# K's chunks with the first fold block and seven variance tiles between them, the constant row's steps beside M's blocks, and another order of the loop's prologue

## The reference

```python
# layer 0
c   = einsum('bct,bcd->bdt', x, W[cond])                 # a 64x64 matrix picked per batch
q   = c @ Wq.T;  router: top 8 of 256 keys, softmax      # aux_out = probs @ aux_values @ Wvd.T @ Wvu.T
u   = clip(0.5 * log1p(var(c)) / mean(log1p(var(c))) + 2.5 * sigmoid(gelu(c @ Wu1.T + bu1) @ Wu2.T), 0, 5)
x1  = x + c + gate(u) * aux_out
# layer 1
r   = x1 @ base_weight.T + base_bias + (x1 @ A[id].T) @ B[id].T
out = x1 + r @ W_base.T + b_base + 0.5 * fourier(sum over 3 experts of masked coefs @ enc @ r)
```

## Time and profile before

| | |
|---|---|
| median of 3 runs | 1653.04 us (1652.23 to 1653.7) |
| the profiled execution's own time | 1652.13 us |
| its span | 1650.3 us |
| PE busy | 1596.8 us, 97% |
| DVE, ACT, POOL busy | 726.9, 587.6, 402.9 us |
| granted PE clock, mean | 0.985 of full speed |

### The profile page before, as it was taken

The page is one execution under the profiler, slowest core; times in us unless marked ns, Lnnn a source line. Parts: engine busy times, 40 slices in busy tenths (PEclk is TensorE's granted clock), DMA queues, the critical chain, the costliest instruction groups (busy, mean ns, idle before and its releaser), DMA issues.

```text
span 1650.3 us, 26441 instructions
## 1 busy us (share of the span) xinstructions
PE 1596.8 (97%) x7690; PEld 1324.9 (80%) x7690; DVE 726.9 (44%) x2497; ACT 587.6 (36%) x1269; POOL 402.9 (24%) x219
## 2 busy tenths in 40 slices
PE   5898999889999999999999999999999999999998
PEld 2676888668888888888888888888888888888886
DVE  3887555544433333333344433333443333433333
ACT  2333343333333333333333333333333333333332
POOL 2787777211111111111111111111111111111110
PEclk9799999999999999999999999999999999999999
DMA  9466655522222322223222222222222222222221
GB/s 338 141 212 215 184 184 167 176 62 86 86 86 89 90 86 84 85 87 91 88 86 84 84 84 84 84 84 84 84 84 84 84 84 84 84 85 85 86 69 49
DMA packets 160287, 176.46 MB, mean 107 GB/s; under 512 B 104654, under 2 KB 123041, under 8 KB 160138
## 3 DMA queue, kind: packets, MB, share of 16 engines
q1 hardware_dynamic: 158498, 170.98, 34.2%
q10 hardware_dynamic: 1768, 5.24, 0.9%
HBM read 136.69 MB, written 39.32 MB: 107 GB/s over the span
## 4 chain that ended last, share of the span: by engine, by line
PE 90%; POOL 3%; issue 3%; DVE 2%; DMA 1%; ACT 1%; SPq 0%; POOLq 0%; DVEq 0%; ACTq 0%
PE pair L1173 43%; PE pair L74 10%; PE pair L75 9%; PE pair L76 9%; PE pair L1142 6%; PE pair L1150 5%; POOL v_lo L220 3%; PE pair L1116 1%; PE pair L1191 1%; PE pair L1190 1%; PE pair L1198 1%; DMA w_kinds<-w_kinds_sb 1%; PE pair L1131 1%; POOL blk_lo L582 1%; PE pair L1121 0%
## 5 line engine op out<-in xcount | busy, mean ns | idle before, releaser
L1173 PE MATMUL pair<-m_hi,t_xt_hi 128*128 128x512 f32 x1024 | 332.4, 406 | 0.0
L1173 PE MATMUL pair<-m_lo,t_xt_hi 128*128 128x512 f32 x1024 | 322.6, 396 | 0.0
L1173 PE MATMUL pair<-m_hi,t_xt_lo 128*128 128x512 f32 x1024 | 321.9, 395 | 0.0
L1018 POOL TENSOR_TENSOR t_narrow<-t_a_raw,t_narrow 128x256 fp32r<-128x256 f32 x64 | 46.8, 731 | 1109.4 <-ACT t_xt_hi L926 1109.4
L1173 PEld LDWEIGHTS pair<-m_hi,t_xt_lo 128*128 128x128 f32 x1024 | 192.6, 188 | 47.0
L1173 PEld LDWEIGHTS pair<-m_lo,t_xt_hi 128*128 128x128 f32 x1024 | 192.5, 188 | 45.9
L1173 PEld LDWEIGHTS pair<-m_hi,t_xt_hi 128*128 128x128 f32 x1024 | 180.5, 189 | 34.3
L220 POOL TENSOR_TENSOR v_lo<-v_x,v_hi 128x1024 fp32r<-128x1024 f32 x64 | 159.6, 2504 | 74.9 <-ACT v_hi L214 74.8
L74 PE MATMUL pair<-t_narrow,t_xt_hi 128*128 128x352 f32 x512 | 177.8, 347 | 0.0
L75 PE MATMUL pair<-t_narrow,t_xt_hi 128*128 128x352 f32 x512 | 169.5, 331 | 0.0
L76 PE MATMUL pair<-t_narrow,t_xt_lo 128*128 128x352 f32 x512 | 168.5, 329 | 0.0
(11 more groups left out here) (218 smaller groups left out, 2650.3 us busy)
## 6 DMA issues: line engine op xcount, KB each, us to landing
v_x<-in_x SPq DMA_DIRECT2D x64, 512.0 KB, 3.5
t_xt<-in_x_t SPq DMA_DIRECT2D x64, 512.0 KB, 3.3
out<-t_out_sb SPq DMA_DIRECT2D x64, 512.0 KB, 2.7
t_rhs_b<-bk_hi SPq DMA_DIRECT2D x256, 64.0 KB, 2.3
t_a_raw<-in_lora_a SPq DMA_DIRECT2D x128, 64.0 KB, 2.9
t_bd<-w_kinds SPq DMA_DIRECT2D x128, 64.0 KB, 2.3
t_rhs_c<-bk_lo SPq DMA_DIRECT2D x128, 64.0 KB, 2.2
blk_raw<-in_left_blocks SPq DMA_DIRECT2D x12, 512.0 KB, 4.0
```

What stands on the lines that cost most here:

```text
L1018: pool.tensor_tensor(lora_groups(p, 1), b["a_raw"][:, p], f(lora_groups(p, 0)), ALU.subtract)
L1173: last = pe.matmul(pm_ps[:, c], lhs, m[:, k, c], start=a, stop=z)
```

## The change

1. **Setup.** `k_chunk` uses a single PSUM pair; its two halves and the two halves of `k_sum` signal separately. Between K's chunks PE now does the products of the first fold block (`first_block(k)`, with its result in the other pair) and variance tiles 2 to 8. `cs_hi` stands on ACT ahead of `v_hi` of tile 2. SP's loads are reordered: x of tiles 2, 3 and 4 and the first two left blocks are loaded here. Tile 9's split and block 0's evacuation are at the end of the lists of setup.
2. **Fold.** Blocks 1 to 11 remain, with tile numbers as before. The constant row's steps are beside M's blocks, two in each, after the second and the fourth tile; blocks 1 to 3 have none.
3. **Prologue.** PE forms the constant row after two of the eight `v_chunks`; ACT places it before the splits of Wu1 and Wq; DVE does `a_low(0)` and `a_low(1)` first, the constant row's low part before the router operands, and `wa_split` last. A memset of `rhs_c` moves from DVE to POOL.

```diff
@@ setup, SP
+        load_picked_w(0)
+        load_picked_w(1)
         load_two(kf, "w_base_t", 0, wbase_in)
+        load_rows(2)
+        sp.dma_start(f_["blk_raw"][:], left_block(t, 0)).then_inc(f_["raw_loaded"], 16)
+        load_picked_w(2)
+        load_two(kf, "w_base_t", 1, wbase_in)
         sp.wait_ge(s["w_kinds_ready"], 2)
         sp.dma_start(t["w_kinds"].rearrange("n c k d -> c n k d"), f(w_kinds[:])
                      ).then_inc(g["w_stored"], 16)
+        load_rows(3)
...
+        sp.wait_ge(f_["blo_ready"], 1)
+        sp.dma_start(f_["blk_raw"][:], left_block(t, P * HID)).then_inc(f_["raw_loaded"], 16)
         sp.wait_ge(g["w_stored"], 16)
...
@@ setup, ACT
-        var_hi(act, v, 2, 3, 0, 1)
         act.wait_ge(s["cs_mm_done"], 1)
         act.mul(cs_hi[:], cs_ps[0:RENC, :], 0.5).then_inc(s["cs_hi_ready"], 1)
-        for k in range(KC):
+        rows_high(2)
+        k_high(0)
+        block_high(0)
+        rows_high(3)
+        for k in range(1, KC):
             k_high(k)
...
+            if k >= 3:
+                rows_high(k + 1)
@@ setup, POOL
+        k_low(0)
+        rows_low(3)
+        for k in range(1, KC):
             k_low(k)
...
+            if k >= 3:
+                rows_low(k + 1)
...
@@ setup, PE
         def k_chunk(k):
+            e = slice(k * P, (k + 1) * P)
+            for h, c in enumerate((LEFT, RIGHT)):
+                if k == 0:
+                    pe.wait_ge(s["enc_cs_split"], 2)
+                else:
+                    pe.wait_ge(f_["k_sum_ready"], 2 * k - 1 + h)
+                product3(pe, k_ps[:, c], enc_hi[:, e], enc_lo[:, e], cs_hi[:, c], cs_lo[:, c], True, True
+                         ).then_inc(f_["k_mm_done"], 1)
+
+        def first_block(k):
...
+            for c in (LEFT, RIGHT):
+                last = product3(pe, z0[:, c], f_["blk_hi"][:, 0, k, :], f_["blk_lo"][:, 0, k, :],
+                                k_hi[:, k, c], k_lo[:, k, c], k == 0, k == KC - 1)
...
+        rows_mm(1)
+        k_chunk(0)
+        k_chunk(1)
+        rows_mm(2)
+        k_chunk(2)
+        first_block(0)
+        rows_mm(3)
+        k_chunk(3)
+        first_block(1)
+        for k in range(4, KC):
             k_chunk(k)
+            first_block(k - 2)
+            rows_mm(k)
+        first_block(KC - 2)
+        first_block(KC - 1)
+        rows_mm(8)
@@ fold, DVE
         def const_step(b, q):
...
+            if q % 2 == 0:
+                return
+            k, lo = b - LBLK, q // 2
...
+        for b in range(1, LBLK):
+            one(b, b % 2, bk_lo, bk_hi)
+        dve.wait_ge(g["base_in"], 64)
+        dve.wait_ge(s["k_right"], KC)
+        dve.memset(spacer, 0.0).then_inc(s["c_chain"], 1)
         with dve.Fori(0, KC // 2) as j:
             b = j * 2 + LBLK
-            one(b, 0, *m_rows(b))
-            one(b + 1, 1, *m_rows(b + 1))
+            one(b, 0, *m_rows(b), const_step)
+            one(b + 1, 1, *m_rows(b + 1), const_step)
@@ main, PE
+        v_chunks((0, 1))
         pe.wait_ge(v["v_bn_done"], NT)
-        pe.wait_ge(f_["c_chain"], 2 * KC)
+        pe.wait_ge(f_["c_chain"], 2 * KC + 1)
         for h in range(2):
             c = slice(h * HALF, (h + 1) * HALF)
             last = pe.matmul(pm_ps[:, c], g["ones"][:], g["const_part"][:, c], start=True, stop=True)
         last.then_inc(s["const_done"], 1)
+        v_chunks((2, 3, 4))
+        wa_chunks(0)
...
+        wa_chunks(2)
+        wa_chunks(3)
```

More of the change, by code:

```diff
@@ L506, in row_load @@
             var_load(sp, t, g, v, tile_of(b, q), q)
-        for q in range(PER):
-            row_load(0, q)
-        sp.wait_ge(s["blo_ready"], 1)
-        sp.dma_start(blk_raw[:], left_block(t, P * HID)).then_inc(s["raw_loaded"], 16)
         with sp.Fori(0, NB - 2) as b:
@@ L561, in store @@
                 act.dma_start(t[part][b * P:(b + 1) * P, :], f(src)).then_inc(s["bk_stored"], 16)
-        row_hi(0, 0, 0)
-        for b in range(LBLK):
-            one(b, b % 2, evac_bk(b), old_rows=b > 0)
+        for b in range(1, LBLK):
+            one(b, b % 2, evac_bk(b), old_rows=True)
         store(LBLK - 1)
@@ L594, in one @@
                 row_lo(b + 1, 0, 1 - i)
-        row_lo(0, 0, 0)
-        with pool.Fori(0, NB // 2 - 1) as j:
+        one(1, 1)
+        with pool.Fori(1, NB // 2 - 1) as j:
             b = j * 2
@@ L643, in one @@
                 var_stats(dve, spacer, g, v, tile_of(b, q), (i + q) % 2)
-                if beside is not None and q < PER - 1:
+                if beside is not None:
                     beside(b, q)
@@ L955, in scalar @@
         last.then_inc(s["const_hi_ready"], 1)
+        for p in range(2):
+            act.wait_ge(moved[p], 16)
+        act.copy(wu_groups(0), wu_raw()).then_inc(s["wu_hi_ready"], 1)
+        a_high(2)
+        act.wait_ge(s["wq_in"], 32)
+        act.copy(wq_groups(0, 0), wq_raw(0))
+        act.copy(wq_groups(1, 0), wq_raw(1)).then_inc(s["wu_hi_ready"], 1)
+        a_high(3)
         act.wait_ge(s["v_mm_ready"], 1)
@@ L1223, in vector @@
         dve.wait_ge(v["v_mm_done"], NT)
+        a_low(0)
+        a_low(1)
         dve.wait_ge(v["v_var_ready"], NT)
@@ L1238, in vector @@
         dve.memset(f(b["lhs_c"][:]), 1.0)
[L1240 to L1242 removed]
+        dve.wait_ge(s["router_mm_done"], 1)
+        dve.tensor_copy(wtw, score_ps[0:BOT, 0:2 * BOT]).then_inc(s["wtw_ready"], 1)
         dve.wait_ge(s["wu_hi_ready"], 1)
@@ L1253, in vector @@
         a_low(3)
+        dve.wait_ge(s["const_hi_ready"], 1)
+        for p in range(2):
+            last = dve.tensor_tensor(b["rhs_c"][BOT:BOT + 1, p, :], pm_ps[BOT:BOT + 1, :],
+                                     f(b["rhs_c"][BOT:BOT + 1, p, :]), ALU.subtract)
+        last.then_inc(s["const_placed"], 1)
         dve.wait_ge(s["router_in"], 48)
```

209 lines of the change are left out of this document (102 added, 107 removed).

## The result

The changed kernel takes 1633.72 us (median of 4 runs, 1629.31 to 1634.62) against 1653.03 for the kernel before: ratio 0.9878, 95% interval 0.9859 to 0.9897, 19.3 us faster. The forecast was 1625, with a range of 1616 to 1639. The profiled execution took 1634.62 us, its span is 1632.8.

What follows compares the result with a forecast made beforehand. PE was taken as the bound, busy 1596.8 of 1650.3 us, so only idle and slow-clock time could be won. Terms 23.6 - 3.0 - 2.0 + 9.3 = 27.9 us; 1652.13 - 27.9 + 0.9 = 1625, range 1616 to 1639.

Steps and rivals of the forecast that it cites:

- cs_hi ahead of tile 2: Setup: K's first product at 30.2 in place of 35.98, 5.7 us earlier.
- K, block 0 and tiles: Setup from 30.2: 138 products, 31.4 us, plus 8.9 us of PE waits, so block 1 starts at about 71.
- the clock: K's stretch: one slow spell of 4 to 7 us, perhaps another around tile 4; 3 us lost, ends 0 and 18.6.
- Blocks 1 to 3 should run at M's pace: Fold: without constant steps, 18.14 us a block; block 4 evacuated at 145.9 in place of 169.56 at full clock.
- Constant steps: M's blocks: steps delay v_lo on POOL; PE waits 0.3 us in each of seven blocks, 2.0 in all.
- Prologue: Main loop's prologue: the wait for the constant row goes; 32.0 us in place of 41.5, 9.3 earlier.
- Sum: Whole kernel: 23.6 - 3.0 - 2.0 + 9.3 = 27.9 us gained, giving 1625 us.
- Rival 1: K's stretch: clock stays low through most of it; 1641 slow throughout, 1633 for half, 1637 taken; chance 0.17.
- Rival 3: M's blocks: constant steps make POOL the limit, costing 16.8 us in place of 2; 1640; chance 0.08.
- Rival 4: Prologue gives little because its last wait is then another; gain there 2 us, so 1632; chance 0.07.
- rival 5: M's blocks: slower, each of 16 constant steps costs PE 3.0 us, 48 in place of 2; 1671; chance 0.03.
- The clock holds: K's stretch and block 4: full clock throughout, so 3 us and 1 us come back; 1621; chance 0.15.

Runs made afterwards that it cites:

- a_block_on_act: The changed kernel with the left-block loads of blocks 2 to 11 issued by ACT instead of SP; 1630.67 us (0.9877).
- a_blocks_split: The changed kernel with SP keeping the left-block load of block 2 and ACT issuing those of blocks 3 to 11; 1627.80 us (0.9852).
- a_both: The changed kernel with block 3 to 11 loads on ACT and M's constant steps after the third and fourth tile; 1626.95 us (0.9842).
- after: The profiled execution of the changed kernel itself, nothing altered; 1634.62 us.
- after_again: The changed kernel run and profiled once more, unaltered, as the measure for kernels beside it; 1633.64 us (0.9883).
- b_cs_first: The kernel before with one change, cs_hi made on ACT ahead of the third variance tile's first part; 1647.44 us (0.9968).

## Why the prediction was right or wrong, step by step

- **cs_hi ahead of tile 2: right.** K's first product was forecast at 30.2 and came at 30.25, and alone the swap is worth 5.3 us of the forecast's 5.7.
- **K, block 0 and tiles: nearly right in the sum, not in its terms.** Block 1's first product was forecast at 71, and 74 with the clock. It came at 75.50:

```profile
30.25 0.50 PE L74 MATMUL pair<-cs_hi,enc_hi 40*128 40x512 f32 x1 [0.77 <-DVE cs_lo L518]
...
52.56 0.50 PE L74 MATMUL pair<-v_hi,v_w 128*128 128x512 f32 x1 [1.34 <-POOL v_lo L220]
...
75.50 0.50 PE L74 MATMUL pair<-k_hi,blk_hi 128*128 128x512 f32 x1 [1.66 <-POOL blk_lo L413]
```

  PE's waits were 4.6 us instead of 8.9 (tile 4's 1.34 for 2.6, blk_lo's 1.66 for 1.9, which was close). The clock cost more: 10.2 us at half of it are worth some 5 us, for 3 forecast. The third term the forecast had at nothing. It reckoned 138 products at 0.227 each, but where PE changes between K's products (40 rows) and others (128 rows), the next two start 0.32 and 0.33 us after the one before instead of 0.23. A change between block 0's products and a tile's, both with 128 rows, has no such gap. Start, duration and instruction at one of each kind:

```profile
57.00 0.40 PE L76 MATMUL pair<-k_hi,blk_lo 128*128 128x512 f32 x1
57.23 0.39 PE L74 MATMUL pair<-v_hi,v_w 128*128 128x512 f32 x1
57.46 0.40 PE L75 MATMUL pair<-v_lo,v_w 128*128 128x512 f32 x1
...
58.39 0.39 PE L76 MATMUL pair<-v_hi,v_w 128*128 128x512 f32 x1
58.71 0.49 PE L74 MATMUL pair<-cs_hi,enc_hi 40*128 40x512 f32 x1
59.04 0.39 PE L75 MATMUL pair<-cs_lo,enc_hi 40*128 40x512 f32 x1
```

  The new order has 13 such changes between 30 and 72 us, which makes 2.6 us or a little more; why they cost this no run tells. So two terms were too small and one too large, and that the sum missed by only 1.5 us is luck in part.
- **"Blocks 1 to 3 should run at M's pace": this step failed.** It was argued from DVE, ACT and POOL alone, and SP was counted only for the tiles behind its new wait in setup, "by my count issued over 10 us ahead of use". That count was right: the loads of tiles 5 to 8 were issued at 39.60 to 49.10 us, 11.8 us and more ahead of their v_hi. The wait that mattered was the next one, SP's for blk_lo of block 1 ahead of block 2's load, 10.0 us, which the prediction does not have. From block 1's evacuation to block 4's it took 63.6 us instead of 57.9. Of the 8.2 us by which block 4 (157.08 for 148.9) missed its forecast, 5.7 are here and 2.5 ahead of block 1's evacuation (93.50 for 91). That SP's list was the cause is shown by the kernels that shorten it: blocks 2 and 3 together take 36.0, 37.8 and 38.2 us in `a_block_on_act`, `a_blocks_split` and `a_both`, and 39.3 to 44.5 in seven executions with SP's list unchanged (`after` 41.9, `after_again` 40.1). In the kernel before, with SP's lead intact and no constant steps, they take 36.1. The trace of before held the warning: SP's loads of left blocks in M's stretch lay 18.83 to 18.88 us apart, more than PE's 18.14.
- **Constant steps: the mechanism was right, the term was mis-sized.** Forecast 0.3 us in each of seven blocks, 2.0 in all; measured 0.56 for six of them and nothing for the last, 3.5 in all (130.3 us from block 4's evacuation to block 11's, for 126.8 before). The step after the second tile meets POOL between blk_lo and v_lo, and one of the next two v_lo slips by 1.0 us (5.75 for two against the 4.77 of the earlier trace rows), and PE then waits:

```profile
204.78 1.46 DVE L724 SCALAR_TENSOR_TENSOR const_part<-k_hi,bb,const_part 128x1024 f32<-128x1024 f32 x1
```
```profile
205.11 5.75 POOL L220 TENSOR_TENSOR v_lo<-v_x,v_hi 128x1024 fp32r<-128x1024 f32 x2
```
```profile
208.56 0.50 PE L74 MATMUL pair<-v_hi,v_w 128*128 128x512 f32 x1 [0.33 <-POOL v_lo L220]
```

  The wait shown was 0.33, as forecast; the pace fell by 0.56. The rest is at the same place: the product ahead of this one started at 207.84 and the one behind it at 208.90, so by the starts the first comes 0.49 us late and the next 0.11 more, 0.6 in all. A wait of PE costs more here than the view of waits lists, since that counts from the end which it gives to the product before.
- **Prologue: right.** Forecast 32.0 us from M's last work to the first mixing product, 9.3 less; measured 31.58 (288.58 to 320.16), 9.9 less than the 41.49 of the earlier trace rows; alone it is worth 11.9. New is the first of these two waits:

```profile
301.38 0.69 PE L1142 MATMUL pair<-t_th 48*64 48x128 f32 x2 [2.56 <-DMA t_z<-in_log_rel]
...
320.16 0.39 PE L74 MATMUL pair<-t_pa_hi,t_bd 128*128 128x320 f32 x1 [1.84 <-DVE t_pa_lo L1397]
```

  DVE was forecast to be busy for 23.5 to 24 us, and was for 23.0:

```profile
288.50:320.00 31.50, 27.26 (x108) 20.86 (x106) 23.02 (x45) 15.91 (x19) 5.78 (x4) 0.89 0.71 230
```

- **Sum.** In the profiled execution block 4 is 12.5 us earlier, M's blocks give back 3.5, the prologue brings 9.9: PE goes on 18.9 earlier, for 27.9 forecast, and the span is 17.5 shorter. Of the last 1.4 us, 1.2 are at the very end of the program. From the last t_pm_hi (at 1619.62, in the kernel before at 1638.29) to the end of the span it takes 13.2 us, in the kernel before 12.0, and in `a_blocks_split`, `a_both` and `b_cs_first` 10.4. The clock is at 0.50 in the four microseconds from 1624, and in the kernel before at 0.64 in those from 1643. The change does not touch this place, so this is chance. About a third of the forecast gain is missing, and the time still lies in the range. That it does is owed to the width of the range: its high end was set by rivals 1 and 4, and SP, which took most of what is missing in the fold, is in none of the rivals.
- **Rivals.** Rival 1, the clock low through most of K's stretch, named a real effect: 10.2 of 45 us. Its time for half the stretch, 1633, is close to the one measured, but it is not what happened: in K's stretch the clock took some 2 us more than forecast, of the 10.4 us of gain that are missing in the profiled execution. (By the prediction's own ends half the stretch would be 9.3 in place of 3, 1631.) Rival 3 had the right place and too high a price, 16.8 for 3.5. Rival 4 is out, since the prologue gave 9.9 us, and so is rival 5: a step of 3.2 us costs PE nothing where POOL has room. The rival "The clock holds" rested on the Trainium skill ("TensorE: Matmul & The Clock Gate", Part 1), by which activity releases the clock. In this trace it fell with waits of only 0.77 and 0.61 us ahead, so the full clock read out of it failed; that the clock stayed up in the one profile with 128-row spare products in these waits agrees with the rule itself.

## What to carry to other kernels

When a change speeds up the engine that bounds a stage, count each feeder's list per round against the new pace, the DMA-issuing queue's as well, and ask how much lead it has at the start: in the kernel before, a list of 18.9 us beside an engine's 18.14 stayed hidden while its lead went from 4.6 to 0.9 us over M's blocks (the load at 164.98 ahead of the evacuation at 169.56, that at 259.27 ahead of 260.18), and here it showed as soon as a wait of 10 us and the faster PE had used the lead up. A queue that waits for a buffer blocks every load behind it, so a load with such a wait belongs on another queue, or behind the loads that are due first. And time a large edit apart from the small ones it comes with: here two reorderings brought 17 of 19 us. And hold a stretch that one profile shows against other executions of the same lists: the slow spells here are 3.4 to 10.2 us long, and the late block is not always the same.

## What the runs showed of the hardware that was not expected

- The granted clock fell to 1.2 GHz near 34.8 us, in a stretch where PE had worked with waits of 0.77 and 0.61 us, and stayed there for 10.2 us of busy PE. It fell between 33 and 36 us in each of eight executions with these lists. Where it did so, and for how long, differed between two executions of the same kernel (34.8 to 45.1; about 35 to 42, and again 52 to 62 right behind a wait of 2.0 us).
- PE's products that follow a change between a contraction over 40 rows and one over 128 start 0.32 and 0.33 us apart instead of 0.23, at full clock (58.39, 58.71, 59.04).
- An instruction of DVE with two SBUF operands and a running one of POOL hold each other: the same step took 1.28, 1.46 (at 204.78), 2.63 (at 212.23) and 3.21 us (`a_both`, at 203.67) by what POOL did, and POOL's v_lo 2.4 or 3.4. The Trainium skill ("SBUF — State Buffer", Who interferes with whom) has it that the one that starts first holds the shared ports and the other waits. The trace agrees in direction: the step that began at 203.67 beside a running v_lo took 3.21 us, about 1.9 longer than the 1.28 of the earlier trace rows, and ended past v_lo's end at 205.8.
- SP needs 3.5 to 4.1 us of its own instructions for one tile's three loads with looked-up addresses, and 5.3 to 5.7 where ACT issues two stores of 512 KB beside it (77.56 to 83.30, 98.67 to 104.18, 139.87 to 145.19), without a wait that the trace shows.
